# A decoder layer on one core: q's moves go to ScalarE's queue from the third batch on, and eight orders of work are shifted

## The chip, the cores and the metric

The kernel runs on one core of a Trainium2 chip. A core has five engines, each with its own instruction queue: TensorE (PE) multiplies, VectorE (DVE), ScalarE (ACT) and GpSimd (POOL) work element by element, SyncE (SP) only issues DMA transfers. ScalarE can issue transfers too, and then does nothing else while it issues. The engines wait for each other on semaphores, and each works through its queue in order. The metric is the device time in microseconds (us) of the one core; smaller is better.

## The reference

The input is x and a context, both 16 batches x 256 tokens x 512 features, in fp32. Three blocks, each followed by a layer norm:

```
h = x * rsqrt(mean(x*x) + 1e-6) * norm_w
q, k, v = h @ Wq.T, h @ Wk.T, h @ Wv.T            # 8 heads of 64
q, k = rope(q), rope(k)
f, g, o = sigmoid(h @ Wbeta.T + ..), sigmoid(h @ Wig.T + ..), sigmoid(h @ Wog.T + ..)
step: M = M*f_t + g_t/8 * outer(k_t, v_t);  y_t = (q_t @ M) * o_t
x = layernorm(x + y @ Wout.T + bout)

r_t = 0.9*r_(t-1) + ctx_t*ctx_t                   # cross memory
x = layernorm(x + x*r)

xn = normalize(x)*gamma + beta                    # 8 experts, 512 tokens each
x = layernorm(x + xn + gelu(xe @ w1[e] + b1[e]) @ w2[e] + b2[e])
```

(The last line adds to the block's input; the token blocks go to the experts in a fixed order.)

## The kernel before

Every fp32 product is made of three fp32r products, high x high, high x low and low x high (`exact_product`, lines 87 to 89), so each operand is split into a rounded part and a rest: ACT writes the rounded part, DVE or POOL the rest.

The first part goes over the 16 batches in a software pipeline. `body(b)` of each engine holds the projections of batch b and the attention of batch b - 1. There are bodies -1 to 1 written out, a loop of two bodies at a time (2 and 3, 4 and 5, ... 12 and 13), and bodies 14 to 17 written out. The second part goes over the 8 experts. Each engine's order is written out by hand; there is no scheduler.

In a body of PE, eight slots (`slot`) hold the projections of k, q and v of batch b (`project_share`), and between them the scores k x q of batch b - 1 in four groups (`scores`, lines 1493 and 1495, banks `turn`) and the weighted values (lines 1508 and 1512). Then come the gate products of batch b + 1, `cross_memory` (lines 1565 to 1570, banks `qk_ps`) and the out projection (`project_out`). The first projection of a body writes `qk_ps` and waits until `grow_memory` of ACT (line 688, semaphore `mem_grown`) has read what `cross_memory` left there; `cross_memory` itself waits for `rope_parts` of DVE (lines 1110 and 1111), which reads the projections from `qk_ps`, and for `context_low` of POOL (line 879).

q and k of a batch are rotated in four parts: DVE multiplies (`rope_parts`), POOL combines (`rotate`, lines 903 and 904, semaphore `rot_done`), and SP moves each part by four transfers of 64 KB into `qkT` (`move`, line 440, semaphores `qk_in`). Parts 0 and 1 are k's, parts 2 and 3 are q's; scores of groups 0 and 1 need parts 0 and 2, those of groups 2 and 3 need parts 1 and 3. All 16 transfers of a batch go through SP's queue.

The gates: PE makes the products of batch b + 1, ACT copies one half out (`gate_low`, line 654), DVE adds (`sum_gates`, lines 1045 to 1051), ACT applies the sigmoid (`gate`, line 665) once DVE has done its eight scans of the decays (`scans`, line 1084), and issues one transfer itself (line 667). `grow_memory` is behind `gate` in ACT's queue. `x_low` of POOL (line 856) splits the next batch's input, `add_memory` of DVE (line 1155) multiplies the residual by the cross memory.

In body 15 ACT goes on to the first expert: it rounds the first weights (`split_w1`, line 757), scales the turned tokens (`token_high`, lines 779 and 782), POOL writes the rest of the weights (`first_w1_low`, line 989) and DVE the rest of the tokens (`token_low`, line 1327) between its last scans.

Of the kernel before, what the change touches and what calls it, by code (L numbers as in the profile page):

```python
# [25 lines left out]
P = 128  # L26
B, L, D = 16, 256, 512
NH, DH = 8, 64
HALF = DH // 2
NT = L // P  # L30
KC = D // P
# [8 lines left out]
NB = 2 * NT  # L40
# [58 lines left out]
def layer_program(nc, scope, x, xT, ctx_in, norm_w, wT, wgT, bg, woutT, bout, gamma, beta, w1, b1, w2, b2,  # L99
# [269 lines left out]
    with nc.Block() as block:  # L369

        @block.sync
        def _(sp):
# [60 lines left out]
            def move(b, r):  # L433

                n, g = 1 - r // 2, r % 2
                if r != 1 or b.n == 0:
                    sp.wait_ge(rot_done, b.after(NB, r + 1))
                for c in range(2):
                    for h in range(2):
                        sp.dma_start(qkT[h:P:2, n, 2 * g + c, :], rot_a[r][c * DH:(c + 1) * DH, h, :]).then_inc(qk_in[g], 16)  # L440
# [25 lines left out]
            def body(b):  # L466
# [41 lines left out]
                if b.within(B):  # L508
                    move(b, 0)
                    move(b, 2)  # L510
                    move(b, 1)
                if b.n == B - 1:
                    sp.wait_ge(decay_done, b.after(NH, NH))
                    load_w2(Step(0), 0)
                if b.within(B):
                    move(b, 3)
                if (b + 1).within(B):
# [90 lines left out]
        def _(act):  # L608
# [82 lines left out]
            def scale_x2(b):  # L691

                act.wait_ge(shift_done, b.after(1, 1))
                for j in range(NT):
                    two = sum_of(b)[:, j, :]
                    act.activation(two, two, ACT.Identity, bias=shift[:, j:j + 1],
                                   scale=rstd[:, j:j + 1]).then_inc(x2_done, 1)

            def body(b):
                if (b + 1).within(B) and b.n >= 0:  # L700
# [10 lines left out]
                for c in range(KC):  # L711
                    if (b - 1).within(B):
                        y_high(b - 1, c)
                    if b.n == 1 and c == 0:
                        square_x(b + 1)
                    if b.n == 1 and c == KC - 1:
                        square_ctx(b - 1)
                    if b.n == B and c == 0:
                        split_w2(Step(0), 0)
                        act.activation(warm[:], one[:], ACT.Gelu)  # L720
                    if (b - 2).within(B) and b.n <= B and c == (2 if b.n == B else 0):
                        scale_x2(b - 2)
                    if b.n == B - 1 and c == 2:
                        expert_normalize(Step(0), 0)
                    if b.n == B and c in (1, 3):
                        gelu(Step(0), c // 2)
                if b.n == -1:
                    weights_high(2)
                    square_x(b + 1)
                    weights_high(1)  # L730
                    weights_high(0)
                if (b + 1).within(B):
                    gate_low(b + 1)
                if b.n == -1:
                    x_high(b + 2)
                if (b + 1).within(B):
                    gate(b + 1)
                if b.n == B - 1:
                    split_w1(Step(0), 0)
                    act.wait_ge(e_const_in, 16 * 3)  # L740
                    for k in range(KC):
                        token_high(Step(0), k)
                if (b - 1).within(B):
                    grow_memory(b - 1)
# [76 lines left out]
        def _(pool):  # L821
# [92 lines left out]
            def body(b):  # L914
# [9 lines left out]
                if (b + 1).within(B):  # L924
                    rms_scale(b + 1)
                    if b.n >= 2:
                        x_low(b + 1)
                if b.n == B:
# [20 lines left out]
                if b.within(B):  # L949
                    rotate(b, 2)  # L950
                    rotate(b, 3)
                if b.n == 1:
                    context_low(b - 1)
                if b.n == 0:
# [73 lines left out]
        def _(dve):  # L1028
# [170 lines left out]
            def second(b):  # L1199
# [17 lines left out]
                y_low(b - 1, 2)  # L1217
                rope_parts(b, 2)
                scans(b, 3)
                y_low(b - 1, 3)  # L1220
                rope_parts(b, 3)
                sum_gates(b + 1)
                scans(b, 4, 5, 6, 7)
                add_residual(b - 1, 0)
# [499 lines left out]
```

## Time and profile before

| | |
|---|---|
| three runs | 1275.42, 1277.99, 1280.56 us; median 1277.99 |
| the profiled execution's own time | 1276.48 us |
| its span | 1274.7 us |
| PE busy | 1247.0 us, 98% |
| DVE, POOL, ACT busy | 795.1 (62%), 735.2 (58%), 460.6 (36%) us |
| DMA, mean rate | 141 GB/s |

The span is the time from the first to the last instruction in the profile; the execution's own time is 1.8 us longer. Busy is the time in which an engine computes; waiting and issuing transfers is not counted. PE is busy in nearly all of the span, so what matters is when PE stands idle, and whom it waits for. The ends of PE's multiplications are modelled, so small idle times can be hidden between them: the start of one batch's first projection to the next one's is the safer measure of a body. The granted clock of PE is 1.00 in nearly all windows, and 0.50 in two short ones.

### The profile page before, as it was taken

To read this page: it belongs to the slowest core of one execution; us is meant where nothing else is said; L and a number is where in the kernel's file an instruction comes from. 1 tells how busy PE (TensorE), PEld (TensorE's weight loads), DVE (VectorE), ACT (ScalarE), POOL (GpSimd) and SP (SyncE) were. 2 spreads that over 40 slices of the span, in tenths; PEclk is the share of its full clock that TensorE was granted. 3 is DMA by queue.
4 is the path that set the end of the run, shared out by engine and by line. 5 is a ranking of instruction groups with operands and counts; after the bars stand their busy time and mean duration, and the time that the engine had idled before them with its cause. 6 is when DMAs were issued, how large, how long until landed. Compare 5 with 4: busy or idle time off the path is not lost.

```text
span 1274.7 us, 19312 instructions
## 1 busy us (share of the span) xinstructions
PE 1247.0 (98%) x6682; PEld 1014.2 (80%) x6682; DVE 795.1 (62%) x1297; ACT 460.6 (36%) x629; POOL 735.2 (58%) x519
## 2 busy tenths in 40 slices
PE   8989999999999999989999999999999999999998
PEld 7768878787878788758888888888888888888886
DVE  5888888888888888953453544534634635435324
ACT  5223333333332332442544434433534344343330
POOL 4866665656565665638538457275294385473651
PEclk9999999999999999989999999999999999999999
DMA  8787777877867776436407316235154073063310
GB/s 282 163 159 141 151 157 152 157 159 156 160 154 158 154 154 126 133 133 223 132 1 272 99 66 218 88 122 183 68 200 171 0 271 99 32 243 98 105 61 33
DMA packets 178107, 179.52 MB, mean 141 GB/s; under 512 B 44732, under 2 KB 121484, under 8 KB 178060
## 3 DMA queue, kind: packets, MB, share of 16 engines
q1 hardware_dynamic: 177548, 178.64, 52.3%
q8 instruction: 29, 0.48, 0.2%
q10 hardware_dynamic: 512, 0.26, 0.1%
q14 instruction: 18, 0.15, 0.0%
HBM read 137.55 MB, written 17.18 MB: 121 GB/s over the span
## 4 chain that ended last, share of the span: by engine, by line
PE 79%; DVE 9%; issue 5%; DMA 3%; POOL 1%; SPq 1%; DVEq 1%; ACT 0%; POOLq 0%; ACTq 0%
PE qk_ps L87 7%; PE qk_ps L89 7%; PE qk_ps L88 7%; PE v_ps L87 6%; PE v_ps L89 6%; PE v_ps L88 6%; PE gate_ps L87 5%; PE gate_ps L89 5%; PE gate_ps L88 5%; PE s_ps L87 3%; PE s_ps L89 3%; PE s_ps L88 3%; PE y_ps L87 3%; PE y_ps L89 3%; PE y_ps L88 3%
## 5 line engine op out<-in xcount | busy, mean ns | idle before, releaser
L1002 POOL TENSOR_TENSOR w_lo<-w_raw,w_hi 128x2048 fp32r<-128x2048 f32 x31 | 143.4, 4625 | 101.2 <-ACT w_hi L757 101.2
L1338 DVE CAST hid_hi<-gate_ps 128x512 fp32r<-128x512 f32 x62 | 42.8, 690 | 196.6 <-ACT gate_ps L797 190.5
L994 POOL TENSOR_TENSOR w_lo<-w_raw,w_hi 128x2048 fp32r<-128x2048 f32 x32 | 148.1, 4627 | 13.6 <-ACT w_hi L767 13.6
L87 PE MATMUL qk_ps<-xT_parts,wqkv_hi 128*128 128x256 f32 x512 | 148.6, 290 | 4.0 <-ACT c_both L688 3.9
L1084 DVE TENSOR_TENSOR_SCAN decays<-f_all,diag 128x384 f32<-128x384 f32 x128 | 150.1, 1211 | 0.6
L89 PE MATMUL qk_ps<-xT_parts,wqkv_lo 128*128 128x256 f32 x512 | 145.0, 283 | 0.0
L88 PE MATMUL qk_ps<-xT_parts,wqkv_hi 128*128 128x256 f32 x512 | 144.8, 283 | 0.0
L1338 DVE CAST hid_hi<-v_ps 128x512 fp32r<-128x512 f32 x62 | 42.8, 690 | 148.2 <-ACT v_ps L797 148.2
L797 ACT ACTIVATE v_ps<-v_ps,b_cols 128x512 f32<-128x512 f32 x64 | 42.4, 662 | 197.9 <-PE v_ps L89 197.9
L87 PEld LDWEIGHTS qk_ps<-xT_parts,wqkv_hi 128*128 128x128 f32 x512 | 96.9, 189 | 13.9 <-issue 7.9
L903 POOL TENSOR_TENSOR rot<-rot 128x256 f32<-128x256 f32 x64 | 62.6, 978 | 74.8 <-DVE rot L1111 74.4
L797 ACT ACTIVATE gate_ps<-gate_ps,b_cols 128x512 f32<-128x512 f32 x64 | 42.1, 659 | 175.9 <-PE gate_ps L89 175.6
L87 PE MATMUL gate_ps<-xnT_hi,w_hi 128*128 128x512 f32 x256 | 101.2, 395 | 0.0
L87 PE MATMUL v_ps<-xnT_hi,w_hi 128*128 128x512 f32 x256 | 100.8, 394 | 0.3 <-issue 0.3
L89 PE MATMUL gate_ps<-xnT_hi,w_lo 128*128 128x512 f32 x256 | 100.7, 393 | 0.0
L966 POOL TENSOR_TENSOR rstd_b<-mean_var_b,ln_eps_b 128x4 f32<-128x4 f32 x15 | 3.0, 201 | 169.3 <-DVE mean_var_b L1314 166.3
L89 PE MATMUL v_ps<-xnT_hi,w_lo 128*128 128x512 f32 x256 | 100.6, 393 | 0.0
L88 PE MATMUL gate_ps<-xnT_lo,w_hi 128*128 128x512 f32 x256 | 100.5, 393 | 0.0
L88 PE MATMUL v_ps<-xnT_lo,w_hi 128*128 128x512 f32 x256 | 100.3, 392 | 0.0
L88 PEld LDWEIGHTS qk_ps<-xT_parts,wqkv_hi 128*128 128x128 f32 x512 | 97.0, 190 | 1.2
L89 PE MATMUL qk_ps<-w_hi,hid_lo 128*128 128x512 f32 x248 | 97.4, 393 | 0.0
L88 PE MATMUL qk_ps<-w_lo,hid_hi 128*128 128x512 f32 x248 | 97.3, 392 | 0.0
(238 smaller groups left out, 3239.6 us busy)
## 6 DMA issues: line engine op xcount, KB each, us to landing
w_raw<-in_w SPq DMA_DIRECT2D x64, 1024.0 KB, 7.4
f_all<-f_dram SPq DMA_DIRECT2D x16, 1024.0 KB, 4.9
qkT<-rot SPq DMA_DIRECT2D x256, 64.0 KB, 2.0
xT_raw<-in_xT SPq DMA_DIRECT2D x16, 512.0 KB, 12.9
x_both<-in_x SPq DMA_DIRECT2D x16, 512.0 KB, 11.6
f_all<-f_dram SPq DMA_DIRECT2D x16, 512.0 KB, 6.1
c_both<-in_ctx_in SPq DMA_DIRECT2D x16, 512.0 KB, 13.5
x_both<-x_dram SPq DMA_DIRECT2D x8, 1024.0 KB, 4.8
```

The costliest lines, as they stand in the source:

```text
L87: eng.matmul(out, lhs_hi, rhs_hi, start=first, stop=False)
L88: eng.matmul(out, lhs_hi, rhs_lo, start=False, stop=False)
L89: return eng.matmul(out, lhs_lo, rhs_hi, start=False, stop=last)
L797: act.activation(up_ps[c % 2][:], up_ps[c % 2][:], ACT.Gelu, bias=b1_cols[:, bass.ds(e.after(FC, c), 1)]).then_inc(gelu_done, 1)
L903: pool.tensor_tensor(a[:, 0, :], a[:, 0, :], s[:, 1, :], ALU.subtract)
L966: pool.tensor_tensor(e_rstd[n][:], e_mean_var[n][:, :, 1], e_ln_eps[:], ALU.add).then_inc(e_var_eps[n], 1)
L994: pool.tensor_tensor(w2_lo[s % 2][:], w2_raw[s % 2][:], w2_hi[s % 2][:].bitcast(F32), ALU.subtract)\
L1002: pool.tensor_tensor(w1_lo[s % 2][:], w1_raw[s % 2][:], w1_hi[s % 2][:].bitcast(F32), ALU.subtract)\
L1084: dve.tensor_tensor_scan(decays[:, n, :], f_all[:, n, :], diag[:], 0.0, ALU.mult, ALU.add).then_inc(decay_done, 1)
L1338: dve.tensor_copy(high, up_ps[c % 2][:]).then_inc(hid_hi_done, 1)
```

## The change

Eight things change. In bodies 2 to 15 q's two parts are moved by ACT (`move_q`): four transfers behind `y_high` of the last values and ahead of `gate_low`, four between `gate_low` and `gate`. SP keeps k's two parts; the second now waits for three rotations instead of none of its own, and in body 15 both stand ahead of the load of the first w2. From body 2 on, POOL's `x_low` waits for `add_memory` (`u_done`). In body 1, ACT does `square_ctx` one step earlier and `grow_memory` ahead of `gate`; POOL does `context_low` between the rotations 2 and 3; DVE takes `y_low` of the last part ahead of a scan and the four last scans ahead of `sum_gates`. In body 16 ACT rounds the first w2 behind the first gelu.

```diff
--- before.py
+++ after.py
@@ -433,7 +433,9 @@
             def move(b, r):
 
                 n, g = 1 - r // 2, r % 2
-                if r != 1 or b.n == 0:
+                if b.n >= 2:
+                    sp.wait_ge(rot_done, b.after(NB, (1, 3)[r]))
+                elif r != 1 or b.n == 0:
                     sp.wait_ge(rot_done, b.after(NB, r + 1))
                 for c in range(2):
                     for h in range(2):
@@ -507,13 +509,10 @@
                     load_w1(Step(0), 0)
                 if b.within(B):
                     move(b, 0)
-                    move(b, 2)
                     move(b, 1)
                 if b.n == B - 1:
                     sp.wait_ge(decay_done, b.after(NH, NH))
                     load_w2(Step(0), 0)
-                if b.within(B):
-                    move(b, 3)
                 if (b + 1).within(B):
                     following(b + 1)
 
@@ -696,6 +695,13 @@
                     act.activation(two, two, ACT.Identity, bias=shift[:, j:j + 1],
                                    scale=rstd[:, j:j + 1]).then_inc(x2_done, 1)
 
+            def move_q(b, g):
+
+                act.wait_ge(rot_done, b.after(NB, 3 + g))
+                for c in range(2):
+                    for h in range(2):
+                        act.dma_start(qkT[h:P:2, 0, 2 * g + c, :], rot_a[2 + g][c * DH:(c + 1) * DH, h, :]).then_inc(qk_in[g], 16)
+
             def body(b):
                 if (b + 1).within(B) and b.n >= 0:
                     if b.n >= 1:
@@ -713,10 +719,9 @@
                         y_high(b - 1, c)
                     if b.n == 1 and c == 0:
                         square_x(b + 1)
-                    if b.n == 1 and c == KC - 1:
+                    if b.n == 1 and c == 2:
                         square_ctx(b - 1)
                     if b.n == B and c == 0:
-                        split_w2(Step(0), 0)
                         act.activation(warm[:], one[:], ACT.Gelu)
                     if (b - 2).within(B) and b.n <= B and c == (2 if b.n == B else 0):
                         scale_x2(b - 2)
@@ -724,15 +729,23 @@
                         expert_normalize(Step(0), 0)
                     if b.n == B and c in (1, 3):
                         gelu(Step(0), c // 2)
+                    if b.n == B and c == 1:
+                        split_w2(Step(0), 0)
                 if b.n == -1:
                     weights_high(2)
                     square_x(b + 1)
                     weights_high(1)
                     weights_high(0)
+                if 2 <= b.n <= B - 1:
+                    move_q(b, 0)
                 if (b + 1).within(B):
                     gate_low(b + 1)
+                if 2 <= b.n <= B - 1:
+                    move_q(b, 1)
                 if b.n == -1:
                     x_high(b + 2)
+                if b.n == 1:
+                    grow_memory(b - 1)
                 if (b + 1).within(B):
                     gate(b + 1)
                 if b.n == B - 1:
@@ -740,7 +753,7 @@
                     act.wait_ge(e_const_in, 16 * 3)
                     for k in range(KC):
                         token_high(Step(0), k)
-                if (b - 1).within(B):
+                if (b - 1).within(B) and b.n != 1:
                     grow_memory(b - 1)
                 if b.n == B - 1:
                     square_ctx(b)
@@ -924,6 +937,7 @@
                 if (b + 1).within(B):
                     rms_scale(b + 1)
                     if b.n >= 2:
+                        pool.wait_ge(u_done, (b - 2).after(NT, NT))
                         x_low(b + 1)
                 if b.n == B:
                     pool.wait_ge(u_done, (b - 2).after(NT, NT))
@@ -948,9 +962,9 @@
                     expert_scale(Step(0), 0)
                 if b.within(B):
                     rotate(b, 2)
+                    if b.n == 1:
+                        context_low(b - 1)
                     rotate(b, 3)
-                if b.n == 1:
-                    context_low(b - 1)
                 if b.n == 0:
                     pool.wait_ge(decay_done, 2)
                     residual(b)
@@ -1216,11 +1230,11 @@
                 scans(b, 2)
                 y_low(b - 1, 2)
                 rope_parts(b, 2)
+                y_low(b - 1, 3)
                 scans(b, 3)
-                y_low(b - 1, 3)
                 rope_parts(b, 3)
+                scans(b, 4, 5, 6, 7)
                 sum_gates(b + 1)
-                scans(b, 4, 5, 6, 7)
                 add_residual(b - 1, 0)
                 add_residual(b - 1, 1)
                 norm_stats(b - 1, 0)
```

In the program order below, each row is an instruction with the line of its kernel, what it writes, `<-`, what it reads, and the size; REGISTER_ALU rows only compute semaphore values. First, ACT's queue in the first body of the loop, from the last value part to the end of the gates, before:

```order
L648 ACTIVATE yT_hi<-s_ps 128x256
L651 REGISTER_ALU
L654 ACTIVATE gates_sum<-gate_ps 24x256
L659 REGISTER_ALU
L661 REGISTER_ALU
L665 ACTIVATE gates<-gates_sum,gate_bias 24x256
L667 DMA f_dram<-gates 16x256
```

The same place in the changed kernel:

```order
L647 ACTIVATE yT_hi<-s_ps 128x256
L700 REGISTER_ALU
L703 DMA qkT<-rot 64x256 x4
L650 REGISTER_ALU
L653 ACTIVATE gates_sum<-gate_ps 24x256
L700 REGISTER_ALU
L703 DMA qkT<-rot 64x256 x4
L658 REGISTER_ALU
L660 REGISTER_ALU
L664 ACTIVATE gates<-gates_sum,gate_bias 24x256
L666 DMA f_dram<-gates 16x256
```

Four transfers came ahead of `gate_low`, four ahead of the sigmoid. Next, ACT's queue at the end of body 1, before; `c_both` from `c_both` and `ctx_parts` are `square_ctx`, `c_both` from `qk_ps` is `grow_memory`:

```order
L648 ACTIVATE yT_hi<-s_ps 128x256
L676 ACTIVATE c_both<-c_both,memory_raw 128x512 x2
L680 ACTIVATE ctx_parts<-c_both 128x1024
L654 ACTIVATE gates_sum<-gate_ps 24x256
L665 ACTIVATE gates<-gates_sum,gate_bias 24x256
L667 DMA f_dram<-gates 16x256
L688 ACTIVATE c_both<-qk_ps,one,memory_raw 128x512 x2
```

In the changed kernel:

```order
L675 ACTIVATE c_both<-c_both,memory_raw 128x512 x2
L679 ACTIVATE ctx_parts<-c_both 128x1024
L647 ACTIVATE yT_hi<-s_ps 128x256
L653 ACTIVATE gates_sum<-gate_ps 24x256
L687 ACTIVATE c_both<-qk_ps,one,memory_raw 128x512 x2
L664 ACTIVATE gates<-gates_sum,gate_bias 24x256
L666 DMA f_dram<-gates 16x256
```

`grow_memory` moved ahead of the sigmoid and its transfer, `square_ctx` ahead of the last `y_high`. Last, ACT's queue in body 15 in the changed kernel, from the normalized tokens (`xn`) to the second token part; before, the row of the transfers is not there:

```order
L805 ACTIVATE xn<-x_both,shift_b_134,rstd_b_132 128x512 x4
L647 ACTIVATE yT_hi<-s_ps 128x256
L703 DMA qkT<-rot 64x256 x8
L770 ACTIVATE w_hi_120<-w_raw_116 128x2048
L792 ACTIVATE turn<-turn,beta_sb,gamma_sb 128x512
L795 ACTIVATE xnT_hi_107<-turn 128x512
L792 ACTIVATE turn<-turn,beta_sb,gamma_sb 128x512
```

Eight transfers now stand ahead of the first expert's weights and tokens.

## Rows read from the trace of the kernel before

**Rows 1.** Waits of PE, whole span: total us, times, longest us.

```profile
PE turn L1493 <- DMA qkT<-rot: 5.6, 2, 5.2
PE qk_ps L87 <- ACT c_both L688: 3.9, 1, 3.9
PE qk_ps L1565 <- DVE rot L1111: 3.9, 5, 0.8
```

**Rows 2.** Timeline of PE, bodies 1 to 2: start us, us, instruction, [idle before].

```profile
65.38 0.39 PE L89 MATMUL s_ps<-wout_hi,yT_lo 128*128 128x512 f32 x1
...
67.14 0.47 PE L1565 MATMUL qk_ps<-ctx_parts,sums 128*128 128x512 f32 x1 [1.37 <-issue]
...
72.66 0.58 PE L87 MATMUL qk_ps<-xT_parts,wqkv_hi 128*128 128x256 f32 x1 [3.92 <-ACT c_both L688]
```

**Rows 3.** Windows of PE: stretch, length, PE busy, PEclk granted, DMA.

```profile
72.60:75.50 2.90, 2.84 (x12) 0.50 0.38 57
...
548.60:553.50 4.90, 4.86 (x20) 0.51 0.73 240
```

**Rows 4.** Timeline of PE: first projection of bodies 3, 4, 5 and 15.

```profile
106.60 0.29 PE L87 MATMUL qk_ps<-xT_parts,wqkv_hi 128*128 128x256 f32 x1
...
139.06 0.29 PE L87 MATMUL qk_ps<-xT_parts,wqkv_hi 128*128 128x256 f32 x1
...
172.76 0.29 PE L87 MATMUL qk_ps<-xT_parts,wqkv_hi 128*128 128x256 f32 x1
...
502.30 0.29 PE L87 MATMUL qk_ps<-xT_parts,wqkv_hi 128*128 128x256 f32 x1
```

**Rows 5.** Timeline of DVE: `add_memory` in bodies 3 and 4.

```profile
110.03 1.42 DVE L1155 SCALAR_TENSOR_TENSOR res<-res,mean_var,c_both 128x512 f32<-128x512 f32 x2
...
142.90 3.54 DVE L1155 SCALAR_TENSOR_TENSOR res<-res,mean_var,c_both 128x512 f32<-128x512 f32 x2
```

**Rows 6.** Timeline of POOL: `x_low` in body 4.

```profile
143.45 2.44 POOL L856 TENSOR_TENSOR xT_parts<-xT_raw,xT_parts 128x1024 fp32r<-128x1024 f32 x1
```

**Rows 7.** Timeline of ACT, end of body 3.

```profile
132.27 0.37 ACT L654 ACTIVATE gates_sum<-gate_ps 24x256 f32<-24x256 f32 x1 [0.68 <-PE gate_ps L1418]
136.09 0.51 ACT L665 ACTIVATE gates<-gates_sum,gate_bias 24x256 f32<-24x256 f32 x1 [3.45 <-DVE decays L1084]
...
137.14 1.45 ACT L688 ACTIVATE c_both<-qk_ps,one,memory_raw 128x512 f32<-128x512 f32 x2 [0.54 <-ACT gates L665]
```

**Rows 8.** Timeline of DVE, end of body 3: `sum_gates` begins.

```profile
133.18 0.40 DVE L1045 TENSOR_TENSOR gates_sum<-gate_ps,gates_sum 24x256 f32<-24x256 f32 x1
```

**Rows 9.** Timeline of SP, end of body 3: q's part 2 is issued.

```profile
132.15 1.10 SPq L440 DMA_DIRECT2D qkT<-rot  x2
```

**Rows 10.** Line 440, 70 to 520 us: count, ns min/median/max, first and last start.

```profile
L440 SPq DMA_DIRECT2D qkT<-rot x213: 461/597/1907, 69.9 to 519.7; - x107
```

**Rows 11.** Line 667, transfers issued by ACT, 100 to 510 us.

```profile
L667 ACTq DMA_DIRECT2D f_dram<-gates x13: 308/309/359, 104.0 to 499.8; - x13
```

**Rows 12.** Page, DMA issues: count, KB each, us to landing.

```profile
f_all<-f_dram SPq DMA_DIRECT2D x16, 512.0 KB, 6.1
```

**Rows 13.** Timeline of SP, body 1: the decays' rows are issued.

```profile
74.05 0.58 SPq L411 DMA_DIRECT2D f_all<-f_dram  x1
```

**Rows 14.** Timeline of DVE, body 2: the decays' rows are first used.

```profile
85.60 0.07 DVE L1076 MEMSET f_all<- 128x8 f32 x1
```

**Rows 15.** Timeline of PE, body 16: first and third group of scores.

```profile
537.34 0.49 PE L1493 MATMUL turn<-qkT 64*128 64x128 f32 x4 [0.76 <-issue]
...
548.64 0.80 PE L1493 MATMUL turn<-qkT 64*128 64x128 f32 x4 [5.23 <-DMA qkT<-rot]
```

**Rows 16.** Timeline of ACT, body 15: first w1 rounded.

```profile
529.16 1.90 ACT L757 ACTIVATE w_hi<-w_raw 128x2048 fp32r<-128x2048 f32 x1
```

**Rows 17.** Timeline of POOL, body 15: rest of the first w1.

```profile
531.14 4.70 POOL L989 TENSOR_TENSOR w_lo<-w_raw,w_hi 128x2048 fp32r<-128x2048 f32 x1 [0.54 <-ACT w_hi L757]
```

**Rows 18.** Timeline of DVE, body 15: the seventh scan.

```profile
533.57 3.09 DVE L1084 TENSOR_TENSOR_SCAN decays<-f_all,diag 128x384 f32<-128x384 f32 x1
```

## The prediction, made before the changed kernel was timed

> **What bounds the kernel now.** I read the page's table first: PE is busy in 98% of the span, so no engine can give back more than PE's idle time, about 28 us. The list of PE's waits says where most of it lies [rows 1]: 5.6 us for moves of q and k, 3.9 us once for `grow_memory`, and five waits of up to 0.8 us for DVE's `rope_parts`. The timeline of PE places the first two: between bodies 1 and 2 [rows 2] and in body 16 [rows 15]. After each of these PE's clock is granted at half, 1.2 GHz, for 2.9 and 4.9 us [rows 3]. At full clock the work in them would take half as long, so the slow clock costs at most 1.45 and 2.45 us; I take 1.2 and 2.2, since the stretches also hold the starts of the work. Last, the starts of the bodies [rows 4]: body 3 takes 139.06 - 106.60 = 32.46 us, body 4 takes 33.70. The short length is PE's own work without a wait; the long one comes in five even bodies (4 to 12), 1.2 us each.
>
> **Part 1, body 1 into body 2.** PE ends `project_out` at about 65.6, waits 1.37 us for `context_low`, and after `cross_memory` 3.92 us for `grow_memory`, which stands in ACT's queue behind a sigmoid that waits for eight scans [rows 2]. Now `context_low` comes one rotation earlier, and POOL should end it at about 65.4; `grow_memory` follows `cross_memory` directly. The first half of `cross_memory` ends about 0.7 us after its start, `grow_memory`'s first half takes another 0.8, and the rest of `cross_memory` covers that: PE should start body 2 at about 67.3 instead of 72.66. With the slow clock gone: -5.4 - 1.2 = -6.6 us. If POOL's `context_low` is slowed by the scans that DVE now does beside it, as far as `x_low` and `add_memory` slow each other below (2.1 us), -4.5 is left; the other end is -6.8. I take -6.6.
>
> What is late next: SP is not earlier in body 1. It issues the decays' rows for batch 2 at 74.05 as before [rows 13], they land about 6 us later [rows 12], at 80.1 to 80.7, and DVE, now 6.6 us earlier than its 85.60 [rows 14], wants them at 79.0 or a little earlier. Its wait delays the rest of its body: +1.4 us (0 to 1.8).
>
> **Part 2, x_low behind add_memory.** In body 3 `add_memory` takes 1.42 us, in body 4 it takes 3.54 [rows 5], and there POOL's `x_low` runs from 143.45 to 145.9 beside it [rows 6]; DVE goes on just after `x_low` ends. The 2.1 us make the rest of DVE's body late, up to `rope_parts`, for which `cross_memory` waits. With `x_low` behind `add_memory` all bodies look like body 3: 5 x 1.2 = -6.0 us. The bounds are -6.0 and 0 (were the cause another). `x_low` itself ends 1.7 us later, but `norm_scale` behind it waited for DVE anyway and so starts earlier than before, and PE needs the split input only at the body's end.
>
> **Part 3, q's moves on ACT.** SP issues q's part 2 at 132.15 in body 3, at once when the rotation is done [rows 9]; one such issue takes 0.46 us after an idle time and 0.60 behind another [rows 10], so four end about 2.4 us later. ACT is free then and waits for the same rotation, so its `gate_low` starts at about 134.7 instead of 132.27 [rows 7], and DVE's `sum_gates`, which began at 133.18 [rows 8], begins at about 135.1: 1.95 us late. From there to the sigmoid DVE's work runs without a gap, 136.09 - 133.18 = 2.9 us, so the sigmoid comes at 138.05. The four moves of q's part 3 between `gate_low` and the sigmoid end at about 137.6 and are covered. `grow_memory` starts 1.05 us after the sigmoid [rows 7], and its first half, 0.73 of the 1.45 us, and the way to PE let PE go 0.83 us later. That is 139.9, and PE wants to start the next body at 139.06 [rows 4]. Before there was 1.1 us to spare; now 0.85 us are missing. DVE's own delay is covered, since before the end of its body it waits for the out projection, which PE ends only at the next body's start; and a stall of PE does not help the chain catch up, since DVE's part of it hangs on PE's second group of scores, a fixed time behind the body's start. The wait stands at the start of bodies 3 to 15: 13 x 0.85 = +11.0 us.
>
> No row shows such a move on ACT's queue. From below: ACT's own transfer takes 0.31 us [rows 11]; at that price four take 1.5 us, and the wait is gone, 0. From above: 1907 ns is the longest issue of line 440 [rows 10], which would make a wait of several us in each body, over 60 in all, though the median says that it is rare. I take the value of the same instruction on SP, 0.60.
>
> SP now issues k's second part at the same moment. In the trace ACT's transfer falls in the midst of SP's moves, and takes 308 to 359 ns all the same [rows 11], so the two queues hardly hold each other up. The Trainium skill (Perfetto Trace Analysis, section "DMA Instruction — HWDGE (DVE, Sync)") speaks against it: the unit that makes the descriptors is locked for one issuer, and the lock wait counts in the issue's time. If the lock were held for the whole 0.60 us, the rows should show issues of 0.6 and more on ACT; they don't, but that transfer has 16 rows and a move has 64. It is a rival.
>
> SP gains nothing that counts: next in its queue stand the rows of the gates, which wait for the sigmoid.
>
> **Part 4, body 15 and 16.** The 5.23 us wait for q's part 3 [rows 15], which stood behind a wait and a 1 MB load in SP's queue, goes, with 2.2 us of slow clock. But ACT now issues eight moves, 5.0 us, ahead of the first expert's weights: line 757 starts at 534.4 instead of 529.16 [rows 16], POOL's 4.70 us on the rest of them run from 536.4 to 541.0 instead of from 531.14 [rows 17]. Before, DVE's seventh scan took 3.09 us [rows 18] and ended at 536.66, 0.8 us after that POOL instruction ended at 535.84: it stood still beside it, and 0.8 us is the scan itself. Now the token parts, next in ACT's queue, are later by the same 5 us, the scan again falls beside POOL's instruction and ends at about 541.8, and the second token part behind it, which frees the banks for the scores, at about 542.5. So the first scores start there instead of at 537.34 [rows 15], after some 6 us of idle PE and with a slow clock of their own, and the third group at about 550. The point to compare is 548.64 + 2.2 = 550.8: the gain is about 0.5 us. If the scan slips in ahead of POOL or ACT is quick, up to -5; if the later load of the first w2 also holds up the first down projection, +2. I take -0.5. The later rounding of w2 in body 16 lies behind the gelu and ahead of a need at about 560: nothing.
>
> **The sum.** -6.6 + 1.4 - 6.0 + 11.0 - 0.5 = -0.7 us against the profiled execution's own 1276.48, hence 1275.8. That execution is 1.5 us below the median of the three runs, 1277.99, which themselves differ by 5.1. I say 1276. What a measurement of this kernel can tell from no change is about 0.5%, 6.4 us.
>
> **The rivals.**
>
> A, the new wait does not come: ACT issues a move in less than about 0.45 us. For it: its own transfer at 0.31 [rows 11], and SP's 0.46 when it is fresh [rows 10]. Against it: the 0.60 of a row of them. All but the 11.0 us stay: 1276.5 - 11.7 - 1 to 2 for the end, 1264.
>
> B, slower: ACT's and SP's moves hold each other up. It decides when an issue takes over 0.8 us beside the other's. Each further 0.25 us on an issue is 1.0 us on the first four, and so 13 us over the bodies; with 0.25 it is 1289, with the whole 0.60 in turn (2.3 us a body) it is 1306. For it: the two queues start at the same semaphore, each with four moves. Against it: rows 11. By the Trainium skill's lock rule alone it would be the 1306.
>
> C, `x_low` is not the cause of the long even bodies, or DVE and POOL collide elsewhere (with the scans beside `o_tables`): the 6 us stay, 1282.
>
> D, the changed orders in bodies 1 and 15 don't do what they say because POOL and DVE hold each other up there: 4 us less of the first gain, 1280; it mixes with the others and gets no chance of its own.
>
> **The chances.** The forecast 0.47, A 0.25, B 0.18, C 0.10. The forecast's own range is 1269 to 1283. To hold 8 in 10 the range takes in A's 1264 and the nearer half of B: 1262 to 1291. Faster by over 0.5% is A and a part of the forecast, 0.31; within 0.5% is most of the forecast and of C, 0.45; slower is B and the upper edge of the others, 0.24.
>
> **What would show it.** In PE's waits the 3.9 us for `grow_memory` and the 5.2 us for the moves are gone; instead some 13 waits for line 687 of the changed kernel, 0.6 to 1.1 us each, and one of 4 to 6 us ahead of the first scores of body 16. `add_memory` takes 1.4 us in every body. The bodies are all of 33.1 to 33.5 us. ACT's moves (line 703) have a median of 0.6 us: at 0.4 or less A is right, at 0.8 or more B. Wrong altogether I am if bodies 3 to 15 start without a wait although the moves take 0.6, or if PE waits in the loop for something else.

## The result: 1279.5 us, and the profile after

| | before | after |
|---|---|---|
| median of 17 runs each, us | 1277.2 (1275.05 to 1280.56) | 1279.5 (1276.94 to 1284.04) |
| span of the profiled execution, us | 1274.7 | 1278.7 |
| start of body 2, of body 3, us | 72.66, 106.60 | 69.13, 106.65 |
| bodies 3 to 14, us each | 32.98 | 33.31 |
| start of body 15 to the end of the span, us | 772.4 | 772.3 |

The ratio to before is 1.0021, with an interval of 1.0011 to 1.0030: slower by 2.3 us. I had forecast 1276, worked out as a gain of 0.7 us on the profiled execution. The time lies in the range (1262 to 1291) and within the 0.5% that I called no change, but the sign is the other one. What went wrong most is one term of the sum, the +1.4 us for what is late next after the start of body 2; the other terms came out near their values. Lines after have other numbers: 687 is `grow_memory` (688 before), 703 q's moves on ACT, 442 the moves on SP, 653 `gate_low`, 664 the sigmoid, 1507 the scores (1493 before), 1579 `cross_memory` (1565 before), 1169 `add_memory`, 1098 the scans.

The waits of PE after (total us, times, longest us), which answer to [rows 1]:

```profile
PE qk_ps L87 <- ACT c_both L687: 8.5, 13, 1.8
PE turn L1507 <- issue: 5.3, 1, 5.3
...
PE s_ps L1522 <- DVE probs L1134: 1.1, 1, 1.1
...
PE qk_ps L1579 <- DVE rot L1125: 1.0, 2, 0.8
...
PE turn L1507 <- DMA qkT<-rot: 0.9, 1, 0.9
```

The wait of 3.9 us is gone, and so are the waits for `rot` in the five even bodies from 4 on; one of 0.78 us for `rot` is new, in body 2. In their place stand the 13 waits for line 687 and a wait of 5.3 us ahead of the first scores of body 16.

The timeline of PE after, at the starts of `cross_memory`, of the first scores and of the bodies (start us, us, instruction, [idle before]), answers to [rows 2, 4]:

```profile
67.56 0.47 PE L1579 MATMUL qk_ps<-ctx_parts,sums 128*128 128x512 f32 x1 [0.71 <-issue]
...
69.13 0.39 PE L87 MATMUL qk_ps<-xT_parts,wqkv_hi 128*128 128x256 f32 x1
...
71.74 0.49 PE L1507 MATMUL turn<-qkT 64*128 64x128 f32 x4 [0.92 <-DMA qkT<-rot]
...
95.01 0.65 PE L1522 MATMUL s_ps<-probs,v 128*64 128x256 f32 x4 [1.07 <-DVE probs L1134]
97.73 0.50 PE L1579 MATMUL qk_ps<-ctx_parts,sums 128*128 128x512 f32 x1 [0.78 <-DVE rot L1125]
...
106.65 0.39 PE L87 MATMUL qk_ps<-xT_parts,wqkv_hi 128*128 128x256 f32 x1 [1.83 <-ACT c_both L687]
...
140.17 0.39 PE L87 MATMUL qk_ps<-xT_parts,wqkv_hi 128*128 128x256 f32 x1 [0.67 <-ACT c_both L687]
173.14 0.38 PE L87 MATMUL qk_ps<-xT_parts,wqkv_hi 128*128 128x256 f32 x1 [0.41 <-ACT c_both L687]
```

The 3.92 us at the start of body 2 are gone, but body 2 itself, from 69.13 to 106.65, now holds four waits, of 0.92, 1.07, 0.78 and 1.83 us: 4.60 in all. So body 3 starts at 106.65, against 106.60 before. (This execution was 1.58 us behind the other one ahead of all edits of body 1, as told below, so that some 1.5 us of the gain are left.)

The bodies of the loop are not all alike. From these starts and the following ones the odd ones of bodies 3 to 12 take 33.5 us and the even ones 32.95, and the waits ahead of them alternate between some 0.4 and 0.65 us; 33.31 is the mean of bodies 3 to 14. Before, it was 32.46 and 33.7 the other way round.

The windows of PE after (stretch, length, busy time of PE, PEld, DVE, ACT and POOL, granted clock, DMA share, GB/s) answer to [rows 3]:

```profile
71.00:76.00 5.00, 4.26 (x36) 3.94 (x37) 4.80 (x12) 3.59 (x8) 3.56 (x4) 1.00 0.34 86
...
546.00:551.00 5.00, 4.80 (x16) 3.14 (x18) 3.78 (x7) 2.81 (x4) 0.00 (x0) 0.50 0.00 0
```

The clock in body 2 is full now. In body 16 half the clock, 1.2 GHz, is granted again, after the wait of 5.3 us.

What those waits come from is seen on DVE (first fence: the scans of body 1, the decays' rows and the rows of the sums of squares in body 2) and on SP (second fence: the decays' rows, the store of the sums of squares and their spread to rows):

```profile
64.34 6.63 DVE L1098 TENSOR_TENSOR_SCAN decays<-f_all,diag 128x384 f32<-128x384 f32 x4
...
82.91 0.07 DVE L1090 MEMSET f_all<- 128x8 f32 x1 [0.80 <-DMA f_all<-f_dram]
...
102.88 0.41 DVE L1065 TENSOR_TENSOR gates_sum<-gates_sum,rms_rows 24x256 f32<-24x256 f32 x1 [1.64 <-DMA rms_rows<-rms_dram]
```

```profile
75.38 0.57 SPq L411 DMA_DIRECT2D f_all<-f_dram  x1
...
84.28 0.81 SPq L396 DMA_DIRECT2D rms_dram<-rms  x2
...
93.01 2.59 SPq L402 DMA_DIRECT2D rms_rows<-rms_dram  x1
```

Against the start of body 2, SP issues the decays' rows at +6.2 us and the spread at +23.9 (before: 74.05 - 72.66 = +1.4 [rows 2, 13], and +17.8). The gates' sum needs the spread near the end of the body, and the sigmoid and `grow_memory` stand behind it. The wait of 0.80 us is the only one of over 0.3 us that DVE has from the scans at 64.34 to its gates' sum at 100.83: while PE waits for `probs` and for `rot`, DVE is busy, and late.

The end of bodies 3 and 4, ACT in the first fence and DVE in the second, answers to [rows 7, 8]; body 3 starts at 106.65, body 4 at 140.17:

```profile
135.33 0.38 ACT L653 ACTIVATE gates_sum<-gate_ps 24x256 f32<-24x256 f32 x1 [3.61 <-POOL rot L917]
...
138.33 0.51 ACT L664 ACTIVATE gates<-gates_sum,gate_bias 24x256 f32<-24x256 f32 x1 [2.62 <-DVE decays L1098]
...
165.55 2.69 ACTq L703 DMA_DIRECT2D qkT<-rot  x4
168.41 0.38 ACT L653 ACTIVATE gates_sum<-gate_ps 24x256 f32<-24x256 f32 x1 [3.17 <-POOL rot L917]
168.50 2.41 ACTq L703 DMA_DIRECT2D qkT<-rot  x4
171.27 0.51 ACT L664 ACTIVATE gates<-gates_sum,gate_bias 24x256 f32<-24x256 f32 x1 [2.49 <-DVE decays L1098]
...
172.31 1.44 ACT L687 ACTIVATE c_both<-qk_ps,one,memory_raw 128x512 f32<-128x512 f32 x2 [0.53 <-ACT gates L664]
```

```profile
135.74 0.41 DVE L1059 TENSOR_TENSOR gates_sum<-gate_ps,gates_sum 24x256 f32<-24x256 f32 x1 [2.17 <-ACT gates_sum L653]
...
168.82 0.41 DVE L1059 TENSOR_TENSOR gates_sum<-gate_ps,gates_sum 24x256 f32<-24x256 f32 x1 [2.17 <-ACT gates_sum L653]
```

From the start of body 3 `gate_low` comes at +28.68 (before, in body 3, +25.67), `sum_gates` at +29.09 (+26.58) and the sigmoid at +31.68 (+29.49): 3.01, 2.51 and 2.19 us later. In body 4 they come at +28.24, +28.65 and +31.10: 2.57, 2.07 and 1.61 us later than in body 3 before. The second row of four moves fits between `gate_low` and the sigmoid.

All issues of the two lines of moves (ns min/median/max, first and last start), and `add_memory` in body 4, which answers to the second of [rows 5]:

```profile
L703 ACTq DMA_DIRECT2D qkT<-rot x112: 468/618/1432, 97.8 to 537.5; - x112
```

```profile
L442 SPq DMA_DIRECT2D qkT<-rot x144: 461/597/2139, 28.9 to 534.6; - x144
```

```profile
143.79 1.40 DVE L1169 SCALAR_TENSOR_TENSOR res<-res,mean_var,c_both 128x512 f32<-128x512 f32 x2
```

Last the tail of body 15, ACT, POOL, DVE and PE in turn, which answers to [rows 15 to 18]; body 15 starts 4.07 us later than before (506.37 against 502.30):

```profile
533.34 4.76 ACTq L703 DMA_DIRECT2D qkT<-rot  x7
538.20 1.92 ACT L770 ACTIVATE w_hi<-w_raw 128x2048 fp32r<-128x2048 f32 x1 [4.65 <-issue]
```

```profile
540.20 4.51 POOL L1003 TENSOR_TENSOR w_lo<-w_raw,w_hi 128x2048 fp32r<-128x2048 f32 x1 [5.30 <-ACT w_hi L770]
```

```profile
542.02 3.49 DVE L1098 TENSOR_TENSOR_SCAN decays<-f_all,diag 128x384 f32<-128x384 f32 x1
```

```profile
546.20 0.80 PE L1507 MATMUL turn<-qkT 64*128 64x128 f32 x4 [5.32 <-issue]
```

### The profile page after: what moved, and what is told of

Same layout as the page of the kernel before. It is cut to its first block, busy times and chain, and to the rows that moved or that the text cites. A ratio compares the mean times of both kernels' runs of the same rounds, so it can differ in the third digit from the quotient of the medians.

```text
span 1278.7 us, 19331 instructions
## 1 busy us (share of the span) xinstructions
PE 1248.3 (98%) x6682; PEld 1012.1 (79%) x6682; DVE 780.3 (61%) x1297; ACT 460.7 (36%) x629; POOL 735.3 (58%) x519
## 4 chain that ended last, share of the span: by engine, by line
PE 57%; DVE 2%; POOL 1%; issue 1%; DMA 0%; ACT 0%; ACTq 0%; POOLq 0%; SPq 0%; DVEq 0%
PE v_ps L87 5%; PE qk_ps L87 5%; PE qk_ps L89 5%; PE qk_ps L88 5%; PE v_ps L89 5%; PE v_ps L88 5%; PE gate_ps L87 5%; PE gate_ps L89 5%; PE gate_ps L88 5%; PE s_ps L87 2%; PE s_ps L89 2%; PE s_ps L88 2%; PE y_ps L87 2%; PE y_ps L89 2%; PE y_ps L88 2%
```

## The experiments

Twelve kernels ran, in three groups of four, each group with runs of before beside it. Two theories stood at the start. The first: the moves on ACT cost about 11 us through the sigmoid, `x_low` gives back about 6, and the missing rest is body 2. The rival, B of the prediction: the two queues hold each other up, wherever the moves stand.

**r1: all moves on SP again, in the order of before, all else as changed.**

```
-                    move(b, 1)          # k alone on SP
+                    move(b, 2)          # q back on SP
+                    move(b, 1)
...
-                    move_q(b, 0)
-                    move_q(b, 1)
```

> The changed kernel with all of q's and k's moves on SyncE again, in the order of the kernel before; the other edits stay. If ScalarE's four moves ahead of gate_low are what holds the bodies back, the bodies 3 to 14 fall from a mean of 33.3 us (the changed kernel) to 32.46 each, the 13 waits for grow_memory (8.5 us) are gone, and the 5.2 us wait in body 16 is back while the 5.3 us wait ahead of its first scores goes: about 1268 us against 1277 before. If instead DVE or POOL holds the bodies back and the moves only happen to fall there, the waits turn into others and it stays at 1276 or more.

Measured: 1268.5 us, ratio to before 0.9935 (0.9921 to 0.9948). That is 11.0 us under the changed kernel, the price forecast for part 3. Bodies 4 to 14 take 32.4 us, PE waits for `grow_memory` once, and the wait for q's moves in body 16 is back at 4.96 us:

```profile
PE turn L1497 <- DMA qkT<-rot: 6.7, 3, 5.0
...
PE qk_ps L87 <- ACT c_both L688: 0.9, 1, 0.9
```

**r2: before with the moves of q and k in their new order, and nothing else.**

```
+                if 2 <= b.n <= B - 1:
+                    move_q(b, 0)        # ACT, around gate_low
...
+                    move_q(b, 1)
```

> The kernel before with nothing but q's moves on ScalarE and SyncE's order of the changed kernel. If the gain of the other edits and the price of the moves simply add up, this is the kernel before plus the price: 13 bodies of 33.3 us or more instead of 32.46 or 33.70, about 1287 us. If x_low's collision and the new wait overlap (both make the sigmoid late), it is 1282 or less.

Measured: 1294.7 us, ratio 1.0141 (1.0125 to 1.0157), a miss by some 8 us. The moves alone cost 18, not 11. The trace shows why the two terms do not add up. Here a body takes 34.3 us, and `add_memory` is slowed by `x_low` in each of the bodies 3 to 6 (3.55, 2.63, 3.54 and 3.55 us), while before, in the same bodies, it was so only in the even ones. PE's waits:

```profile
PE qk_ps L87 <- ACT c_both L687: 12.7, 14, 3.9
PE qk_ps L1575 <- DVE rot L1121: 8.2, 11, 0.8
```

Both waits stand in one body, one behind the other.

**r3: the changed kernel, with `x_low` free to start ahead of `add_memory`.**

```
-                        pool.wait_ge(u_done, (b - 2).after(NT, NT))
                         x_low(b + 1)
```

> The changed kernel without x_low's wait for add_memory. If x_low beside add_memory makes DVE's body late, add_memory takes 3.5 us again in some bodies, q's second part comes 1 to 2 us later there, and the wait for grow_memory grows by as much: 6 us or more slower than the changed kernel, about 1285 to 1290. If the new wait does nothing, it stays at 1279 to 1280.

Measured: 1287.0 us, ratio 1.0085 (1.0070 to 1.0100). So part 2 is worth 7.5 us in this kernel. The row of `add_memory` in body 4, and PE's waits:

```profile
143.58 3.54 DVE L1168 SCALAR_TENSOR_TENSOR res<-res,mean_var,c_both 128x512 f32<-128x512 f32 x2
```

```profile
PE qk_ps L1578 <- DVE rot L1124: 9.7, 13, 0.8
PE qk_ps L87 <- ACT c_both L687: 8.7, 13, 1.5
```

1.40 us became 3.54 by that one wait, and the wait for `rot` is in all 13 bodies. r2 and r3 show the same: once each body waits for `grow_memory`, the collision is there in odd bodies too. The edits are not independent.

**r4: the changed kernel with body 1 in the orders of before.**

```
-                if b.n == 1:
-                    grow_memory(b - 1)   # ACT: ahead of the sigmoid
...
-                    if b.n == 1:
-                        context_low(b - 1)   # POOL: ahead of rotate(b, 3)
...
-                scans(b, 4, 5, 6, 7)     # DVE
                 sum_gates(b + 1)
+                scans(b, 4, 5, 6, 7)
```

(`square_ctx` and the last `y_low` go back too.)

> The changed kernel with the orders of body 1 of the kernel before (square_ctx, grow_memory, context_low, y_low and the four scans). By my prediction these edits give 6.6 less 1.4 us, so this would be 5.2 us slower, 1284.7. The trace of the changed kernel says otherwise: body 2 starts 5.1 us earlier after its own start is taken off, but body 3 only 1.5 us; if SyncE's queue at the end of body 1 (rows of the decays, the tables of o, rms) sets body 3's start, this kernel is only 1 to 2 us slower than the changed one, about 1281.

Measured: 1281.8 us, ratio 1.0037 (1.0023 to 1.0050). Part 1 is worth 2.3 us by the medians, where the forecast had 5.2 (6.6 less 1.4), which would be 1284.7. The size is rough: the interval of this ratio and that of the changed kernel (1.0011 to 1.0030) overlap, but the forecast's 1284.7, a ratio of 1.0059 to 1277.2, lies outside. The rows of this run do not price part 1 more closely. They are of its slowest execution (1283.67), in which the half clock at the start of body 2 lasts for 5.4 us, from 74.80 to 80.20 (granted clock 0.50), instead of 2.9 [rows 3]. So this is the part of the sum that failed. All its edits were taken back together here; none was tried by itself.

**r5: r1, and in body 15 SP issues all moves ahead of its wait for the scans and the load of the first w2.**

```
                     move(b, 1)
+                    move(b, 3)
                 if b.n == B - 1:
                     sp.wait_ge(decay_done, b.after(NH, NH))
                     load_w2(Step(0), 0)
-                if b.within(B):
-                    move(b, 3)
```

> As the run before, and in body 15 SyncE issues all 16 moves ahead of the wait for the scans and the load of the first w2. If the 5.2 us wait in body 16 came only from that order in SyncE's queue, it goes with the 2.2 us of half clock behind it: 7 us less than the run before, about 1261 us. If the load of w2 or the first w1 is what is late next, less than 3 us are gained.

Measured: 1260.5 us, ratio 0.9873 (0.9858 to 0.9888), the fastest of all: 16.7 us under before, 19.0 under the changed kernel. The third group of scores in body 16 starts without a wait, and the first only 0.76 us late:

```profile
527.89 0.49 PE L1496 MATMUL turn<-qkT 64*128 64x128 f32 x4 [0.76 <-issue]
...
533.89 0.49 PE L1496 MATMUL turn<-qkT 64*128 64x128 f32 x4
```

So a gain of 8 us at the end was to be had by an order on SP, without ACT.

**r6: of q only the second part on ACT, between `gate_low` and the sigmoid; the first on SP.**

```
-                    move_q(b, 0)         # ahead of gate_low
                     gate_low(b + 1)
                     move_q(b, 1)
```

> The changed kernel with q's first part (rotation 2) back on SyncE, and only q's second part (rotation 3) issued by ScalarE, between gate_low and the sigmoid. If only the four moves ahead of gate_low cost time, the bodies are of 32.4 us and no wait for grow_memory is left in the loop: about 1264 us (four moves instead of eight ahead of the first w1). If any four moves on ScalarE cost the same, the bodies stay at 33.3: about 1275.

**r7: of q only the first part on ACT, ahead of `gate_low`; the second on SP.**

```
                     move_q(b, 0)
                     gate_low(b + 1)
-                    move_q(b, 1)
```

(SP issues q's second part behind k's two.)

> The counterpart: q's first part issued by ScalarE ahead of gate_low, the second by SyncE behind k's. If the place ahead of gate_low is what costs, the bodies are of 33.3 us with 13 waits for grow_memory as in the changed kernel, and only the end gains: about 1275 us. If the cost were the eight issues together, the waits halve: about 1270.

Measured: r6 1266.9 us, ratio 0.9919 (0.9905 to 0.9933); r7 1274.4 us, ratio 0.9977 (0.9965 to 0.9988). Both issue four moves per body on ACT beside SP's. PE's waits of r6 in the first fence, of r7 in the second:

```profile
PE qk_ps L87 <- ACT c_both L686: 1.2, 2, 1.0
```

```profile
PE qk_ps L87 <- ACT c_both L688: 8.4, 13, 1.8
```

The place decides, not the queue: four moves ahead of `gate_low` bring all 13 waits, four behind it bring none after the start of body 4. Bodies 3 to 14 take 32.47 us each in r6, 32.45 in r1 and 33.5 in r7. The profiled execution of r7 is its slowest, and a part of that mean is one longer wait, of 1.84 us at the end of body 5, with half clock behind it (granted 0.50 from 208.5 to 210.5). The medians of r6 and r7 differ by 7.5 us; r7's end, from body 15 on, is 1.6 us shorter than r6's, so the bodies cost somewhat more than that. The median issue on ACT is 622 ns in r6 and 626 in r7. That rules the rival out as the cause of the long bodies.

**r8: r5 with the three constants of the first expert behind the rows of batch 2 in SP's queue.**

```
-                    sp.dma_start(gamma_sb[:], gamma).then_inc(e_const_in, 16)   # and beta, b1
                     following(b + 1)
+                    sp.dma_start(gamma_sb[:], gamma).then_inc(e_const_in, 16)   # and beta, b1
```

> The kernel of 1260.5 us (all moves on SyncE, end reordered) with the three loads of gamma, beta and b1 behind the rows of batch 2 in SyncE's queue instead of ahead of them. If body 2 lasts 36.0 us instead of 32.4 because SyncE's queue brings batch 2's rows and rms late, it gets up to 1.5 us shorter: about 1259. If body 2 is long because the moves of batch 1 land late, or because DVE itself is behind, nothing changes: 1260.5.

Measured: 1261.5 us, ratio 0.9883 (0.9867 to 0.9898): no gain. SP issues the decays' rows at +5.2 us from the start of body 2 instead of +6.4. In both kernels DVE finds them there without a wait, and yet body 2 is 36.4 us long (36.0 in r5). The store of the sums of squares still stands behind the constants, and DVE waits 3.2 us for their spread. So the decays' rows, the one item that my term priced, do not set body 2 in these two kernels.

**r9: r5 with the sums of squares stored at the end of each body, ahead of the o rows (and r8's edit).**

```
                 load_g(b)
+                if (b + 1).within(B):
+                    store_rms(b + 1)
                 spread_o(b)
```

> The fastest kernel so far (all moves on SP, tail reordered: 1260.5), with SP storing the sums of squares of batch b+2 at the end of body b, between the gates' rows and the o rows, instead of at the start of body b+1, and the three constants behind that. Theory: body 2 is long because everything in SP's queue is late against the earlier PE, and the last of it is the spread of the sums of squares (rms_rows), issued at 91.09 because their store went out only at 82.01, though POOL had them at 75.2. Then the store goes out at about 76.4, rms_rows at about 85.5, DVE's wait of 2.80 us is gone and with it PE's 0.93 us at the start of body 3: body 2 is 35.1 us instead of 36.0, 1259.6 in all. Rival: the length comes from the moves and the scans; then body 2 stays at 36.0 and the wait turns into another, 1260.5.

Measured: 1275.5 us, ratio 0.9990 (0.9980 to 0.9999), 15 us worse than r5, where I expected a gain of 0.9. The wait for the spread is gone in body 2, as expected, but body 2 takes 38.0 us and the bodies 3 to 14 33.5 (32.5 in r5). PE now waits in all 13 bodies for `rot`, and POOL, which rotates the o rows, waits 8.93 us for them in body 2 and 7.33 us in body 3:

```profile
PE qk_ps L1568 <- DVE rot L1114: 15.1, 13, 3.5
```

```profile
128.23 1.86 POOL L897 TENSOR_TENSOR rot<-rot,rope_sb 128x512 f32<-128x512 f32 x1 [7.33 <-DMA rot<-o_dram]
```

SP issues those rows from 116.97 on and they are there at 128.23. In r5 they are issued from 109.01 on, each lands 2.0 to 2.9 us after its issue, and POOL uses them at 115.19 without a wait. In front of them now stands the store of the sums of squares. In r5 that store is issued at 82.01, and the spread, which needs it, goes out at 91.09, 9 us later. So the likely reason is that the o rows stand behind a slow store; this was not tried by itself.

**r10: r5 with four moves of batch 1 ahead of the 1 MB of x and xT in body 1, and x ahead of xT.**

```
-                    load_xT(b + 2)
-                    load_x(b + 2)
                     move(b, 2)
+                    load_x(b + 2)
+                    load_xT(b + 2)
```

> The fastest kernel so far, with SP issuing four moves of batch 1 (k's first part) ahead of the two 0.5 MB loads of x and xT in body 1. Theory: PE's wait of 1.16 us for qkT in body 2 is there because these moves share the DMA engines with the 1 MB issued just ahead; then the wait falls to 0.3 or less, and PE is 0.9 us earlier, 1259.6. Rival: the decays (scans of 6.65 us beside POOL) are late as well, DVE's product for the first scores starts at 72.90 either way, and the gain turns into a wait for probs: 1260.5. The loads come 2.5 us later and could make the sums of squares late, then 1261.5.

Measured: 1262.5 us, ratio 0.9889 (0.9875 to 0.9903). The wait for `qkT` in body 2 is gone: in both kernels the four moves go out as soon as their rotation is done, but they land 2.0 to 2.5 us after their issue here, and the same moves behind the 1 MB in r5 up to 5.4 us after. All of the gain and more came back elsewhere. SP's later items slipped by about 0.9 us against the body's start (the spread at +24.5 instead of +23.6) and body 2 grew from 36.0 to 37.7 us. DVE's waits in it:

```profile
DVE gates_sum L1054 <- DMA rms_rows<-rms_dram: 3.6, 1, 3.6
DVE f_all L1079 <- DMA f_all<-f_dram: 2.0, 1, 2.0
```

```profile
94.44 0.65 PE L1511 MATMUL s_ps<-probs,v 128*64 128x256 f32 x4 [2.24 <-DVE probs L1123]
```

**r11: the edits of r9 and r10 together.**

> The two edits together: if both theories hold 1258.7, with body 2 at 34.2 us; if only that of the sums of squares does, 1259.6; if one late chain takes the other's place, 1260.5.

Measured: 1276.0 us, ratio 0.9990 (0.9981 to 0.9999). PE waits for `rot` in all 13 bodies, 16.3 us in all, and POOL for the o rows as in r9: they decide here too.

**r12: the changed kernel with r9's edit.**

> The changed kernel with only the earlier store of the sums of squares (and the constants behind it). Theory: of body 2's 37.52 us the wait of 1.83 us at its end falls to the 0.67 us of the other bodies, body 2 is 36.3 us, 1278.3 in all. Rival: body 2 stays at 37.5, 1279.5. If the earlier store disturbs SP's moves of k in the loop (o rows 0.8 us later), some tenths more in each body, over 1280.

Measured: 1288.5 us, ratio 1.0091 (1.0078 to 1.0104), 9 us over the changed kernel, and with the signs of r9: PE waits for `rot` in 13 bodies, 8.6 us in all, and POOL waits 8.70 us for the o rows in body 2. The expectation named this risk and put some tenths of a us per body on it; bodies 3 to 14 take 34.1 us instead of 33.3, and body 2 takes 39.5 instead of 37.5.

## Why the prediction was wrong, step by step

**Part 1, the start of body 2: right.** Forecast 67.3. The trace shows 69.13, but this profiled execution was already 1.58 us behind the other at the first gate product of body 1 (60.21 against 58.63), ahead of the edits of that body; without that it is 67.55. The slow clock is gone too.

**Part 1, what is late next: this term failed.** I wrote +1.4 us (0 to 1.8), for the decays' rows alone; that one chain made DVE wait 0.80 us. Body 2 took 37.52 us against 33.94 - 1.2 = 32.74 at full clock before; less 0.67 us, the wait that the moves bring at the end of body 3, 4.1 us were lost. Of these 3.93 stand in PE's own four waits (4.60 less 0.67). PE now came 5 us earlier to a body whose inputs did not: of SP's queue I priced the first late item and stopped. Behind it stood the o rows (POOL waits 2.12 us), the sums of squares and their spread (DVE 1.64), and in front of it the moves of batch 1 (PE 0.92). Nor did DVE get away: its four scans of body 1 took 6.63 us beside POOL's `context_low` and rotation, against 3.48 before. I had bounded what this costs POOL (`context_low` took 3.04 us instead of 2.37), not what it costs DVE, which came out of its scans only 1.3 us earlier than before while PE came 5 us earlier. r4 measures the whole of part 1 as some 2.3 us. In r8 the decays' rows come earlier and body 2 gets no shorter; in r10 SP's later items are later still, and body 2 is longer. How much each chain is to blame stays open: when one was taken away (the spread in r9, the moves in r10), another ended last, and no run left DVE's scans where they were with the rest of part 1 in place. The last sign that I had named for being wrong altogether, that PE waits in the loop for something else, did show, in body 2.

**Part 2: right, and worth more than its price.** `add_memory` takes 1.40 or 1.41 us in every body, and the even bodies are no longer the long ones. The forecast took 6.0 us from bodies that did not yet wait for `grow_memory`; in the changed kernel the same wait is worth 7.5 (r3), since without it odd bodies collide as well. In the sum this did no harm, because part 3 was priced with `x_low` already out of the way: 12 bodies grew by 395.70 to 399.72 = 4.0 us, forecast 12 x 0.85 - 6.0 = 4.2.

**Part 3: right in place and mechanism, and in size on the mean.** Issues of 0.62 us, 13 waits, bodies of 33.3 on the mean, and 11.0 us when undone (r1). I forecast 1.95 us for `sum_gates` and for the sigmoid, from body 3. In body 3 they are 2.51 and 2.19 us later, in body 4 2.07 and 1.61, so that the bodies are 33.5 and 32.95 in turn and not all of 33.1 to 33.5; why odd and even ones differ stays open. A single wait is 0.4 to 0.7 us in most bodies, where I had 0.6 to 1.1. The two queues hold each other up only a little: ACT's median is 618 ns, and SP's is 597, as it was before [rows 10]. The medians hide a small price. The first four moves on ACT, beside SP's, take 2.69 us in bodies 3 and 4, the second four, when SP issues nothing, 2.41; in body 3 it is ACT's second issue, 861 ns, that is long. That is rival B at 0.3 us a body instead of its 1.0 or more. The Trainium skill (Perfetto Trace Analysis, section "DMA Instruction — HWDGE (DVE, Sync)") says that the unit is locked for one issuer. This trace bears out no lock for the whole 0.60 us, which would have made the four 2.4 us longer; the 0.3 us, and the longest issues, 1432 and 2139 ns (1907 before, when SP alone made moves), may be such waits.

**Part 4: right.** Forecast in the times of before: `w_hi` at 534.4, POOL's part to 541.0, the scan to 541.8, the first scores at 542.5. With the later start of 4.07 us these are 538.5, 545.1, 545.9 and 546.6; the rows show 538.20, 544.71, 545.51 and 546.20. From body 15's start to the end 0.1 us was gained, forecast 0.5.

**The sum.** With 4.1 in the place of 1.4 it is -6.6 + 4.1 - 6.0 + 11.0 - 0.5 = +2.0 us; the medians differ by 2.3. How close the two are is in part luck: r4's price of part 1 is rough, and the -6.0 and the +11.0 hold only in that order, with `x_low` out of the way first; put into the kernel of before, the moves cost 18 (r2), and taken out of the changed kernel the wait of `x_low` costs 7.5 (r3).

## What to carry to other kernels

When a stall is taken away, the engine arrives earlier at everything behind it. List every input of the next stage with the queue that brings it and the slack that it had, not only the first one that is late; here a gain of 6.6 us was worth some 2.3. One of these moves cost the engine that issued it 0.6 us (ACT's median 618 ns), and what counts is what stands behind it in that engine's order: four moves behind `gate_low` left the bodies as they were (32.47 us in r6, 32.45 in r1), and four ahead of it cost 7.5 us (r7 against r6). And edits that each remove a wait are not additive; price one with the others in place.

## What was not expected of the hardware

- With a store of 2 x 128 single values put ahead of them in SP's queue, the o rows were there 11 us after the first issue (r9), instead of at most 6.2 us (r5). That the store is the cause was not tried by itself.
- DVE's scan, 0.87 us each with POOL idle (3.48 for four, body 1 before), took 1.66 us beside POOL's arithmetic (6.63 for four, body 1 after), and 3.49 us for one beside POOL's long subtraction of w1 in body 15.
- Four moves on ACT took about 0.3 us more while SP issued its own (2.69 against 2.41 us), which the median of the issues (618 ns) does not show.
